# A gated cross-attention and expert kernel: constants in one load behind the key weights, pad rows stored later, and two value products moved among batch 0's head pairs

## The reference, cut to what matters

```python
x = x + tanh(g_xattn) * xattn(layernorm(x), ctx, mask)        # 16 heads of 32
x = x + tanh(g_ffn)   * moe(layernorm(x))                     # 8 experts, top 2

def xattn(hs, ctx, mask):
    q, k, v = hs @ Wq.T + bq, ctx @ Wk.T + bk, ctx @ Wv.T + bv
    s = clip(q @ k.T / sqrt(32)); s = where(mask, s, -10000); s = clip(s, -50, 50)
    delta = rs * ((softmax(s) @ v) @ Wo.T + bo)
    return layernorm(delta) * ln_gamma + ln_beta
```

## Time and profile before

| | |
|---|---|
| median of 3 runs | 956.95 us (953.62 to 959.67) |
| the profiled execution | 953.08 us, its span 951.3 us |
| granted TensorE clock, mean | 0.987 |
| PE busy | 904.9 us, 95% |
| DVE, ACT, POOL busy | 432.6, 383.4, 267.8 us |
| batch 0's part of the span | from about 32 to 80 us |

### The profile page before, as it was taken

How to read it: one execution, slowest core, us unless ns; L and a number is a source line. 1 busy time by engine, 2 the same in 40 slices (tenths; PEclk the granted TensorE clock), 3 DMA queues, 4 the chain that set the end, 5 groups by cost and what they waited for, 6 DMA issues and landing times.

```text
span 951.3 us, 14769 instructions
## 1 busy us (share of the span) xinstructions
PE 904.9 (95%) x4369; PEld 726.9 (76%) x4370; DVE 432.6 (45%) x802; ACT 383.4 (40%) x740; POOL 267.8 (28%) x330
## 2 busy tenths in 40 slices
PE   7978999999699999999999999999999999999994
PEld 7746777778578888888888888888888888888883
DVE  5658868577871221721621635422532172136111
ACT  4485757543332222622622625322622262235221
POOL 6136555564412112212212212211311221212211
PEclk9999999999799999999999999999999999999997
DMA  8210222108272112631631543611551263121121
GB/s 315 90 45 1 78 100 77 56 34 314 99 288 44 23 22 37 208 109 33 203 117 33 189 131 110 221 22 22 170 161 22 37 213 103 33 33 22 33 33 22
DMA packets 27812, 92.90 MB, mean 98 GB/s; under 512 B 5457, under 2 KB 5457, under 8 KB 21137
## 3 DMA queue, kind: packets, MB, share of 16 engines
q1 hardware_dynamic: 18576, 72.03, 20.2%
q0 software_dynamic: 8640, 20.62, 11.8%
q10 hardware_dynamic: 576, 0.02, 0.0%
HBM read 73.98 MB, written 18.68 MB: 97 GB/s over the span
## 4 chain that ended last, share of the span: by engine, by line
PE 80%; issue 6%; POOL 5%; DVE 4%; ACT 3%; DMA 1%; DVEq 0%; SPq 0%; POOLq 0%; ACTq 0%
PE bank L259 71%; PE bank L1612 3%; PE bank L1598 2%; POOL ex_lo L824 2%; POOL o_lo L804 1%; DMA raw<-in_w_attn 1%; PE bank L1415 1%; PE bank L1303 1%; POOL xr L808 1%; ACT g_hi L1216 1%; PE bank L1409 1%; PE bank L1351 0%; DVE tok_tile L691 0%; DMA xg<-h_rows,slot_idx 0%; PE bank L1331 0%
## 5 line engine op out<-in xcount | busy, mean ns | idle before, releaser
L259 PE MATMUL bank<-g_hi,gt_hi 128*128 128x512 f32 x592 | 237.5, 401 | 0.9 <-DVE gt_lo L717 0.9
L259 PE MATMUL bank<-g_lo,gt_hi 128*128 128x512 f32 x592 | 234.1, 395 | 0.0
L259 PE MATMUL bank<-g_hi,gt_lo 128*128 128x512 f32 x592 | 234.1, 395 | 0.0
L747 DVE TENSOR_TENSOR hid<-silu,bank 128x256 f32<-128x256 f32 x148 | 61.4, 419 | 306.9 <-ACT silu L1268 306.9
L1268 ACT ACTIVATE silu<-bank 128x256 f32<-128x256 f32 x148 | 56.5, 382 | 253.0 <-PE bank L259 253.0
L966 POOL COPY g_idx<-slot_idx 128x1 int32 x37 | 6.9, 185 | 470.3 <-ACT w_nxt L1282 470.3
L259 PEld LDWEIGHTS bank<-g_hi,gt_lo 128*128 128x128 f32 x592 | 111.3, 188 | 27.0
L259 PEld LDWEIGHTS bank<-g_hi,gt_hi 128*128 128x128 f32 x592 | 111.3, 188 | 26.3 <-issue 1.1
L259 PEld LDWEIGHTS bank<-g_lo,gt_hi 128*128 128x128 f32 x592 | 111.4, 188 | 25.0
L259 PE MATMUL bank<-dn_hi,hd_hi 128*128 128x512 f32 x296 | 126.8, 428 | 0.0
L259 PE MATMUL bank<-dn_hi,hd_lo 128*128 128x512 f32 x296 | 116.9, 395 | 0.0
(11 more groups left out here) (236 smaller groups left out, 1284.8 us busy)
## 6 DMA issues: line engine op xcount, KB each, us to landing
raw<-in_w_exp SPq DMA_DIRECT2D x48, 1024.0 KB, 5.3
xs<-in_x SPq DMA_DIRECT2D x4, 1024.0 KB, 6.3
out_rows<-xr SPq DMA_DIRECT2D x16, 256.0 KB, 2.1
h_rows<-dh SPq DMA_DIRECT2D x16, 256.0 KB, 2.1
raw<-in_w_attn SPq DMA_DIRECT2D x3, 1024.0 KB, 14.0
xr<-in_x SPq DMA_DIRECT2D x3, 1024.0 KB, 5.8
raw<-in_w_attn SPq DMA_DIRECT2D x4, 256.0 KB, 7.2
rows<-in_b_rows SPq DMA_DIRECT2D x1, 1024.0 KB, 17.6
```

What stands on the lines that cost most here:

```text
L259: mm = eng.matmul(psum, a(k), b(k), start=(first and k == 0 and j == 0), stop=(last and k == n - 1 and j == 2))
L747: dve.tensor_tensor(hid[:, p, :], silu[:, p, :], bank[p][:, 256:512], ALU.mult).then_inc(hid_done, 1)
```

## The change

- The four small loads of ACT become one (`cst`, 47 columns on 128 partitions, 188 bytes each), which ACT issues behind its work on the key weights. `bcol`, `gsc`, `gate_w` and `mask_sb` are now parts of `cst`.
- SP's sixteen-increments of eight semaphores move behind its loads.
- POOL stores the pad rows from `r_two`, in five DMAs in place of three, behind the first inverse root and the constants of the routing. DVE waits for them before it writes `r_two` (`invert_sums`), and ACT's wait is gone.
- PE makes the value products of the blocks 3 and 0 at the old place, and those of 1 and 2 in batch 0: one behind `scores(0, 2)`, one behind `scores(0, 3)`. `scores(0, 1)` stands ahead of `q_product(0, 3)`, `scores(0, 2)` ahead of pair 1, `scores(0, 3)` ahead of pair 3. The 16 transposes of batch 0 stand together. 30 transposes of the identity in place of 36.
- DVE's `q_low(0, 3)` and the bias of the third value product stand behind clip 3, the bias of the fourth and the splitting of `bo` behind clip 5. ACT's `q_high(0, 3)` stands behind `exps(3)`.
- POOL's wait for the scaled bias rows stands behind batch 0.
- Buffers are laid out anew: `wv` shares its space with `dh` and `xr`, the split context with the output weights. SP's load of `xr` for batch 0 waits for the last value product.

```diff
@@ sync
-            for t in range(TT):
-                sp.sem_inc(x1_store[t], 16)
-                sp.sem_inc(h_store[t], 16)
             sp.dma_start(c_raw[:, :, :], ctx_t).then_inc(crload, 16)
...
             sp.dma_start(raw[:, 3, :], w_attn[3]).then_inc(wload[3], 16)
+            for t in range(TT):
+                sp.sem_inc(x1_store[t], 16)
+                sp.sem_inc(h_store[t], 16)
...
+                if not back:
+                    sp.wait_ge(kv_mm, 1 + NB)
                 sp.dma_start(xr[:, :, :], x_b[b]).then_inc(rload, 16)
@@ vector
             def invert_sums(n):
                 dve.wait_ge(den_c, n + 1)
+                dve.wait_ge(pad_store, 80)
...
                 clip(b, 3)
+                if not back:
+                    q_low(b, 3)
+                    v_bias(2, (2,))
                 if front:
                     ln_statistics(b + 1)
...
                 clip(b, 5)
+                if not back:
+                    v_bias(3, (3,))
+                    split_bias()
@@ gpsimd
-            pool.dma_start(out_rows[NT], f32(kbd_hi[:, :, :]).rearrange("p k n -> p (k n)")).then_inc(pad_store, 16)
-            pool.dma_start(h_rows[NT], f32(kbd_hi[:, :, :]).rearrange("p k n -> p (k n)")).then_inc(pad_store, 16)
-            pool.dma_start(pad_cw, f32(kbd_hi[:, 0, 0:E])).then_inc(pad_store, 16)
...
-            pool.wait_ge(dset, 5)
+            for half in range(2):
+                cols = slice(half * (S // 2), (half + 1) * (S // 2))
+                pool.dma_start(out_rows[NT][:, cols], f32(r_two[:, :])).then_inc(pad_store, 16)
+                pool.dma_start(h_rows[NT][:, cols], f32(r_two[:, :])).then_inc(pad_store, 16)
+            pool.dma_start(pad_cw, f32(r_two[:, 0:E])).then_inc(pad_store, 16)
             ex_low(0, 0)
             ex_low(0, 1)
             batch(0, False, True)
+            pool.wait_ge(dset, 5)
@@ scalar
-            act.dma_start(mask_sb[:, :], mask).then_inc(cload, 16)
-            act.dma_start(bcol[:, :, :], b_cols).then_inc(cload, 16)
-            act.dma_start(gsc[:, :], gates.partition_broadcast(P)).then_inc(cload, 16)
-            act.dma_start(gate_w[:, :, :], gate_t).then_inc(cload, 16)
...
                 exps(2)
+                exps(3)
                 if not back:
+                    q_high(b, 3)
                     o_copy(b, 0, back)
-                exps(3)
                 exps(4)
...
+            act.dma_start(cst[:, :], consts).then_inc(cload, 16)
             split_weight(1)
@@ tensor
+            def first_half(b):
+                pv(b, 0, False)
+                scores(b, 2)
+                v_product(1, bank[0])
+                pv(b, 1, False)
+                pv(b, 2, False)
+                scores(b, 3)
+                v_product(2, bank[1])
+                pv(b, 3, False)
+                pv(b, 4, False)
+                pe.wait_ge(kv_sb, 2 + NB + 1)
+                x_transposes(b + 1, range(0, 2))
+                pv(b, 5, False)
+                x_transposes(b + 1, range(2, KC))
...
-            stay_busy(36, bank[3])
+            stay_busy(30, bank[3])
...
-            for i, n in enumerate(V_ORDER):
...
-                product3(pe, bank[2 + n][:, :], lambda k: c_hi[:, k, two], lambda k: c_lo[:, k, two],
-                         lambda k: wv_hi[:, k, :], lambda k: wv_lo[:, k, :]).then_inc(kv_mm, 1)
-                if i >= 2:
-                    if i == 2:
-                        pe.wait_ge(kv_sb, 1)
-                    x_transposes(0, range(2 * i - 4, 2 * i - 2))
+            v_product(3, bank[5])
+            v_product(0, bank[2])
+            pe.wait_ge(kv_sb, 1)
+            x_transposes(0)
             pe.wait_ge(w_lo_done, 2)
             pe.wait_ge(kv_sb, 5)
             q_product(0, 0)
-            pe.wait_ge(kv_sb, 6)
             q_product(0, 1)
-            pe.wait_ge(kv_sb, 2 + NB + 1)
-            first_part(0)
+            scores(0, 0)
+            pe.wait_ge(q_l, 1)
+            q_product(0, 2)
+            scores(0, 1)
+            pe.wait_ge(q_l, 2)
+            q_product(0, 3)
             batch(0, False, True)
```

More of the change, by code:

```diff
@@ L472, in clip, with split_bias, v_bias @@
                                   ALU.min, ALU.max).then_inc(s_clip, 1)
+            def split_bias():
+                dve.wait_ge(gates_ready, 1)
+                dve.tensor_scalar(rows[:, 1, :], rows[:, 1, :], tg[:, 2:3], None, ALU.mult).then_inc(dset, 1)
+                dve.tensor_scalar(rows[:, 2:4, :], rows[:, 2:4, :], tg[:, 0:1], None, ALU.mult).then_inc(dset, 1)
+                dve.wait_ge(dset, 5)
+                dve.wait_ge(setup, 22)
+                dve.tensor_scalar(bo_two[0:1, :], rows[0:1, 1, :], 1.0, None, ALU.mult).then_inc(bo_done, 1)
+                dve.tensor_scalar(bo_two[LO_ROW:LO_ROW + 1, :], rows[LO_ROW:LO_ROW + 1, 1, :], 1.0, None,
+                                  ALU.mult).then_inc(bo_done, 1)
+                dve.wait_ge(bo_done, 2)
+                dve.tensor_tensor(bo_two[LO_ROW:LO_ROW + 1, :], rows[LO_ROW:LO_ROW + 1, 1, :],
+                                  f32(bo_two[LO_ROW:LO_ROW + 1, :]), ALU.subtract).then_inc(bo_done, 1)
+            v_bank = {3: bank[5], 0: bank[2], 1: bank[0], 2: bank[1]}
+            def v_bias(i, places):
+                dve.wait_ge(kv_mm, i + 2)
+                for place in places:
+                    dve.tensor_tensor(v_all[:, place, :], v_bank[V_ORDER[i]][:, :], rows[:, 0, :],
+                                      ALU.add).then_inc(kv_sb, 1)
             def batch(b, back, front):
@@ L535, in _ @@
             split_weight(2)
-            def v_bias(i, places):
-                dve.wait_ge(kv_mm, i + 2)
-                for place in places:
-                    dve.tensor_tensor(v_all[:, place, :], bank[2 + (place - 1) % NB][:, :], rows[:, 0, :],
-                                      ALU.add).then_inc(kv_sb, 1)
             dve.wait_ge(row_load, 16)
@@ L1174, in _ @@
             q_high(0, 2)
-            q_high(0, 3)
             batch(0, False, True)
@@ L1429, in batch @@
                     spread(b - 1, 1)
[L1430 to L1433 removed]
+                    pv(b, 0, back)
                     spread(b - 1, 2)
                     spread(b - 1, 3)
[L1436 to L1437 removed]
+                    pv(b, 1, back)
                     scores(b, 1)
@@ L1440, in batch @@
                     o_product(b - 1, 0)
-                else:
-                    scores(b, 2)
-                pv(b, 2, back)
-                if back:
+                    pv(b, 2, back)
                     scores(b, 2)
@@ L1447, in batch @@
                     o_product(b - 1, 1)
-                pv(b, 3, back)
-                if back:
+                    pv(b, 3, back)
                     o_product(b - 1, 2)
-                else:
-                    scores(b, 3)
-                pv(b, 4, back)
-                if front:
-                    x_transposes(b + 1, range(0, 2))
-                if back:
-                    scores(b, 3)
-                pv(b, 5, back)
-                if front:
-                    x_transposes(b + 1, range(2, KC))
+                    pv(b, 4, back)
+                    if front:
+                        x_transposes(b + 1, range(0, 2))
+                    scores(b, 3)
+                    pv(b, 5, back)
+                    if front:
+                        x_transposes(b + 1, range(2, KC))
+                else:
+                    first_half(b)
                 if back:
```

78 lines of the change are left out of this document (29 added, 49 removed).

## The result

| | before | after |
|---|---|---|
| median of 20 runs each, in turns on one chip | 957.47 us (952.41 to 960.42) | 959.27 us (954.94 to 962.58) |
| the profiled execution | 953.08 us, span 951.3 | 960.70 us, span 959.0 |
| granted TensorE clock, mean | 0.987 | 0.976 |

The ratio after to before is 1.0032, with a 95% interval of 1.0017 to 1.0048: the change costs 3.1 us, 1.6 to 4.6 (the two medians lie 1.8 us apart, inside that). It is within the 1% bound of the forecast, and it is a loss.

A forecast was written before the change was run, and what follows sets the result against it. PE holds 80% of the chain of waits, so the change is worth what it moves batch 0's end: -3.1 (W), -2.3 (Q against W), +6.4 (batch 0) = +1.0 us, median 958.0, range 952.5 to 962.5.

The forecast's parts named there:

- T1: Start of batch 1's first transposes on PE, 59.19 us before; forecast at Q + 33.4 instead of Q + 27.0.
- W: End of the value weights' low part wv_lo, 17.43 us before; forecast 3.1 us earlier.
- the small loads: DMA at the kernel's head: small packets hold up the engines; without them loads behind land 2.3 us earlier.
- SP's 0.55: SP's semaphore increments ahead of its first load; moved behind the loads they give 0.55 us.
- the slow stretch: DMA traffic from 5 to 8 us, 94 GB/s before; forecast to become 422 GB/s, worth 2.3 us.
- The one-to-one alternation in rows 4: 184 small-load packets against 150 weight packets in the slow stretch; taken as evidence that small packets hold up DMA.
- The rival itself, a W of -0.7: Slow DMA stretch at the head has another cause and stays: W gains 0.7, median 960.4; chance 27%.
- Q: Start of batch 0's query products, 32.19 us before; forecast at W + 12.4 = 29.85.
- value products at the start: Two products ahead of batch 0's transposes, which start at W + 7.7; Q follows 4.8 us later, gain 2.3 us.
- batch 0 from Q on: Moved products delay DVE's and ACT's queues; batch 1's transposes at Q + 33.4 instead of Q + 27.0, loss 6.4 us.
- the moved products are hidden: Rival: in batch 0 DVE and ACT catch up, sum -5.4 to -2.2, 951.6 to 954.8 us; chance 13%.
- The step that failed: the clock: Rival: TensorE's clock halves if a gap grows past about 3 us, costing 2 to 4 us, 960 to 962; chance 6%.

The follow-up runs named there:

- e9: e1 with one of its small loads, the three gates, read by all 128 partitions from one address; wv_lo ends at 17.23 us, no median given.
- e10: e7 with the broadcast load of the three gates moved from ACT's head to behind the key weights; wv_lo ends at 15.90 us, no median given.
- e1: The changed kernel with the constants again as four small loads at ACT's head; 961.09 us, ratio 1.003 to the kernel before.
- e3: The changed kernel with identity matmuls as fillers in PE's gaps (ring of splits, scores 3, batch 1's transposes); 956.88 us, ratio 0.9996 to before.
- e8: The changed kernel with SP's semaphore increments put back ahead of its loads; wv_lo ends at 16.21 us, no median given.
- e6: The changed kernel with only DVE's bias of the first moved product put behind clip 5; batch 1's transposes start at 61.93 us, no median given.
- e4: The changed kernel with the second moved product behind pair 4 and the biases behind clips 5 and 7; 954.18 us, ratio 0.9973 to before.
- e11: e4 run again unchanged, in one job with e12; 954.20 us, ratio 0.9988 to before.
- e5: e4 plus identity matmuls (16, 8 and 12) filling PE's gaps around batch 0's transposes; 953.43 us, ratio 0.9985 to before.
- e12: e5 run again unchanged, in one job with e11; 952.21 us, ratio 0.9964 to before.
- e2: The changed kernel with the two value products and their biases back ahead of the query products, scores in new order; 955.15 us, ratio 0.9984 to before.
- e7: The kernel before with only SP's semaphore increments moved behind its loads; wv_lo ends at 16.56 us, no median given.

## Why the prediction was right, and where it was not

**The forecast time, right by two errors that cancel.** Forecast 958.0, measured 959.27. The profiled execution was to take 954.1 and took 960.7: 6.6 us too low. The step from there to the median was to add 3.9, as it did before the change, and took off 1.4: 5.3 us too much. The trace's 953.08 was an execution with a clock of 0.987, and the median of 33 executions of the kernel before is 0.979; over these, the time falls by 5.7 us for 0.01 of clock. So the profile of before showed fewer half-rate stretches than most of its executions have, and the forecast put back in a lump, without knowing it, the clock that it denied the changed kernel. At T1 the forecast was 14.33 + 12.4 + 33.4 = 60.1, and it is 65.5: 1.4 of W, 0.9 and 3.1 of the two parts behind it.

**W, step "the small loads": the wrong cause, half the size.** Forecast -3.1, measured -1.7. SP's 0.55 stands in the issue of the first load (0.81 in place of 1.30). The 2.3 us for the slow stretch were then 1.2: its main cause is the broadcast of the gates at the head (e9, e10), not the number of packets (e1), and the two slow microseconds from 4 to 6 stayed: (422 - 236 + 422 - 147) / 422 = 1.1 us, just what is missing. "The one-to-one alternation in rows 4" was a coincidence in time: small packets ran beside the stretch, and without one load among them most of it goes. The row that spoke for the rival, the 3.4% of the engines in the earlier trace rows, was right about the packets. The rival itself, a W of -0.7, missed by 1.0 the other way. Its cause, the start of many loads at once, may still be behind the two slow microseconds that are left.

**Q, step "value products at the start": right but for the clock.** The first transposes stand at 23.48 = W + 7.75, forecast W + 7.7. From there to Q it is 5.5 us, forecast 4.8: the second eight transposes took 1.97 us at half rate in place of 1.06.

**Batch 0, step "batch 0 from Q on": right.** The statistics take 3.1 us (49.37 to 52.49), the value taken. ACT's copy stands in front of `hs` with 6.19 us of idle time, ended by PE. At full rate the loss is 6.6 (e3, forecast 6.4). The parts of it, each T1 - Q with its half-rate time taken off, which is what Q to scores 0 took over 5.6 us and what the second moved product took over 2.8:

- after: 36.5 - 1.4 - 1.6 = 33.5; e1 and e8, with the same order, give 33.5 too
- without the first bias ahead of the statistics (e6): 33.4 - 1.9 = 31.5
- without the product ahead of pair 3 too (e4): 31.5 - 2.8 = 28.7; e11 gives 28.7, and e5 and e12, at full rate, show 28.8 and 28.7
- with the products back and only the scores in their new order (e2): 29.1 - 1.1 = 28.0, where 1.1 is what pair 3 took longer up to ACT's copy (52.15 to 54.68, and 53.95 to 55.42 in e4)
- before: 27.0

So DVE's queue costs 2.0 us and ACT's 2.8. Of the 1.7 us that are left, 1.0 comes with the new order of the scores, without any moved product (in e2 the copy that `hs` stands behind waits for a pair 3 that now stands behind scores 3), and 0.7 is what two products of 2.8 us each cost in e4's place. As they stand in after, the products cost 33.5 - 28.0 = 5.5 of their 5.6 us: "none is hidden" was right, and the 0.8 us of the 6.4 that the forecast left unnamed is the scores' order. The rival "the moved products are hidden" was wrong for this order, and would have been nearly right for e4's.

**The step that failed: the clock.** The forecast set the rival's point at a gap "past about 3 us", from one gap of 2.93 us that did nothing, and put the loss at nothing for its own shorter gaps. The gaps came as worked out (1.87 and 1.99 us, forecast 2.0; 2.60, forecast 2.7), and the clock fell behind each. It cost 0.9 us ahead of Q, 1.4 in the first query product and 1.6 in the second moved product: 3.9 us of T1 in this execution, 2.4 us in the median (e3 against after, in different jobs).

How far the change's gaps are to blame differs from gap to gap. The one ahead of the first transposes, 1.8 to 1.9 us, stands in six traces (after, e1, e4, e6, e8, e11), and half rate follows in all six; where it is filled or not there (before, e2, e3, e5, e7, e9, e10, e12), the clock from 24 to 32 us is 1.00. The one of 2.0 us ahead of scores 3 was followed by half rate in after, e2 and e9, and not in e1 and e8. And with before's own order in batch 0 the clock can fall too. This is e7, behind idle times of 1.17 and 0.97 us:

```profile
50.00:52.00 2.00, 1.95 (x6) 1.39 (x7) 1.86 (x8) 0.31 (x1) 1.44 (x2) 0.66 0.00 0
52.00:54.00 2.00, 2.00 (x6) 1.20 (x4) 1.06 (x2) 1.26 (x2) 1.24 (x3) 0.50 0.00 0
```

e10 shows the same from 50 to 52 us. So the gap in the ring is a loss that the change brought; of the loss at scores 3 a part can be found in executions of before as well. The rival had 6%. It should have been weighed as something that an idle time of 2 us, or less, can do in some executions.

**Costed at nothing, and at nothing.** The load of `cst` landed 7.1 us behind its issue at 8.98, at 16.1, ahead of `tg` at 18.78. e2 keeps the five pad stores, the one load, the late split of `bo` and the fewer fillers, and is not slower than before.

## What to carry to other kernels

A piece of work moved into gaps is free only if no queue puts it in front of something that others wait for: here 4.8 of 6.5 us came from two places in in-order queues, and went away by moving one product and two biases, no work removed. An experiment that takes the moved work away and keeps the new order (e2) tells the price of the order itself. A gap that opens where TensorE was kept busy is not idle time at no cost, even at 2 us; where the clock's level differs between executions, one profile can't be the base of a sum, and its mean clock should be read beside those of the other runs first. And a load of a few bytes that all partitions read from one address did not belong ahead of the first large loads here; behind them, or as part of a table with a row for each partition, it cost little or nothing.

## What the runs showed of the hardware

- **A broadcast of 12 bytes to 128 partitions** (1.5 KB in all), issued at the head beside the first large loads, took the traffic of 3 us from 313 to 179 GB/s (e1, e9). The same load issued at 9.2 us left it at 412, 437, 344 and 426 (e10). 340 small packets with an address each took nothing (313 both).
- **The clock fell after short gaps.** PE's timeline of after, behind the 1.99 us ahead of scores 3:

```profile
55.28 0.39 PE L262 MATMUL bank<-wv_lo,c_hi 128*128 128x512 f32 x1
55.51 0.42 PE L262 MATMUL bank<-wv_hi,c_lo 128*128 128x512 f32 x1
55.74 0.61 PE L262 MATMUL bank<-wv_hi,c_hi 128*128 128x512 f32 x1
56.15 0.63 PE L262 MATMUL bank<-wv_lo,c_hi 128*128 128x512 f32 x1
...
58.71 0.61 PE L262 MATMUL bank<-wv_lo,c_hi 128*128 128x512 f32 x1
59.13 0.41 PE L262 MATMUL bank<-wv_hi,c_lo 128*128 128x512 f32 x1
```

  The matmuls had run without a pause from 54.04; the half rate came 1.7 us into them and stood until 59.1. In e2 a gap of 1.98 us did the same (clock 0.61 from 50 to 60 us), in e4 one of 1.88 before the first transposes too. Gaps of 2.00 and 1.99 us ahead of scores 3 did nothing in e1 and e8 (clock 1.00 from 54 to 62 us), and 2.93 us did nothing before. What decides between them these runs don't show. The Trainium skill, "TensorE: Matmul & The Clock Gate", Part 1, ties the rate to how busy the array has been of late; that the fall comes while matmuls run, 1.7 us behind the gap's end, is in line with that.
- **The mean clock tells most of the run-to-run spread.** Over 33 executions of the kernel before, in one job, time and mean clock correlate with -0.97.
